# Last scatters waited for on SyncE, one weight subtraction on VectorE, half of the expert bias loaded in the expert stage, and the end of the second attention in another order

## The reference

```python
x = x + _L0_xattn_ref(_layernorm(x), ctx_4096, ctx_4096, ...)   # 8 heads over 64 rows of a batch
x = x + _L0_ffn_ref(_layernorm(x), L0_ffn_W_gate, L0_ffn_b_gate, L0_ffn_W_e, L0_ffn_b_e)
x = x + _L1_xattn_ref(_layernorm(x), ctx_4096, ctx_4096, ...)   # 32 heads, 8 key heads
x = x + _L1_ffn_ref(_layernorm(x), ...)                         # gated, 1376 hidden
```

```python
logits = x @ W_gate + b_gate
_, top_idx = jax.lax.top_k(logits, TOP_K)          # TOP_K = 2
y_all = relu(einsum('bsd,edh->bseh', x, W_e) + b_e)
y = take_along_axis(y_all, top_idx[..., None], axis=2).mean(axis=2)
```

## Time and profile before

| what | value |
|---|---|
| median of 3 runs | 890.0 us (886.49 to 892.05) |
| the profiled execution | 889.12 us |
| its span in the trace | 887.4 us |
| mean granted clock | 0.985 of full speed |
| busy share of PE, DVE, ACT, POOL | 95%, 49%, 39%, 32% |
| PE's share of the chain that ended last | 73% |

### The profile page before, as it was taken

One profiled execution on the slowest core, in us unless ns is written; L12 is line 12 of the kernel. 1 busy time (PEld: TensorE's weight loads), 2 busy tenths in 40 slices (PEclk: granted clock), 3 DMA queues, 4 the chain that ended last, 5 costly groups with the idle time before them and its releaser, 6 DMA issues.

```text
span 887.4 us, 19751 instructions
## 1 busy us (share of the span) xinstructions
...
## 2 busy tenths in 40 slices
...
GB/s 284 131 252 254 229 251 288 171 322 199 166 164 113 197 122 135 170 143 144 118 50 58 137 119 38 45 33 1 18 114 12 1 13 107 0 49 47 1 0 48
DMA packets 55388, 105.28 MB, mean 119 GB/s; under 512 B 8226, under 2 KB 12322, under 8 KB 55042
## 3 DMA queue, kind: packets, MB, share of 16 engines
...
## 4 chain that ended last, share of the span: by engine, by line
PE 73%; POOL 3%; issue 2%; DMA 2%; ACT 1%; DVE 1%; SPq 0%; DVEq 0%; ACTq 0%; POOLq 0%
PE c_ps L1273 9%; PE c_ps L1275 9%; PE c_ps L1274 9%; PE c_bank L1797 4%; PE c_bank L1311 3%; PE c_bank L1312 3%; PE c_bank L1317 3%; PE c_bank L1798 3%; PE c_bank L1803 3%; PE c_bank L1861 3%; PE c_bank L1010 2%; PE c_bank L1011 2%; PE c_bank L1016 2%; PE c_ps L1836 2%; PE c_po L1011 2%
## 5 line engine op out<-in xcount | busy, mean ns | idle before, releaser
L1350 DVE SCALAR_TENSOR_TENSOR d_hid<-c_ps,d_b_up,d_silu 128x512 f32<-128x512 f32 (+1 forms) x44 | 33.0, 751 | 227.9 <-PE c_ps L1275 227.9
L1273 PE MATMUL c_ps<-d_nT_hi,gate_up_hi 128*128 128x512 f32 (+1 forms) x352 | 139.9, 398 | 0.0
L1275 PE MATMUL c_ps<-d_nT_hi,gate_up_lo 128*128 128x512 f32 (+1 forms) x352 | 138.6, 394 | 0.0
L1274 PE MATMUL c_ps<-d_nT_lo,gate_up_hi 128*128 128x512 f32 (+1 forms) x352 | 138.3, 393 | 0.0
L1229 ACT ACTIVATE d_silu<-c_ps,d_b_gate 128x512 f32<-128x512 f32 (+1 forms) x44 | 30.3, 689 | 141.6 <-PE c_ps L1275 141.6
L1189 POOL TENSOR_TENSOR late_x<-late_x,d_b_down 128x512 f32<-128x512 f32 x16 | 20.9, 1340 | 188.8 <-DMA late_x<-x_after_attention 188.8
L1275 PEld LDWEIGHTS c_ps<-d_nT_hi,gate_up_lo 128*128 128x128 f32 (+1 forms) x352 | 65.2, 185 | 16.6
L1274 PEld LDWEIGHTS c_ps<-d_nT_lo,gate_up_hi 128*128 128x128 f32 (+1 forms) x352 | 65.4, 186 | 15.9
L1273 PEld LDWEIGHTS c_ps<-d_nT_hi,gate_up_hi 128*128 128x128 f32 (+1 forms) x352 | 65.3, 185 | 15.4
L1236 ACT ACTIVATE d_hid_hi<-d_hid 128x512 fp32r<-128x512 f32 (+1 forms) x44 | 27.8, 632 | 125.4 <-DVE d_hid L1350 125.4
L1040 ACT ACTIVATE b_rowsT_hi<-c_bank 128x512 fp32r<-128x512 f32 x39 | 23.4, 599 | 77.8 <-PE c_bank L999 77.8
...
## 6 DMA issues: line engine op xcount, KB each, us to landing
...
```

Source lines behind the costliest of these rows:

```text
L1273: pe.matmul(bank[0:w, :], gu_hi[:, cols], nT_hi[:, g % 2, k, :], start=k == 0, stop=False)
L1274: pe.matmul(bank[0:w, :], gu_hi[:, cols], nT_lo[:, g % 2, k, :], start=False, stop=False)
L1275: mm = pe.matmul(bank[0:w, :], gu_lo[:, cols], nT_hi[:, g % 2, k, :], start=False, stop=k == KD - 1)
```

## The change

- At the start SP issues the six loads of the output projection's constants (`load_o_consts`, L288 to L291) before, no longer after, the loads of ctx(1) and x(2).
- bias(0) is no longer loaded in the first block. SP issues it in the expert stage between the loads of the rows of blocks 1 and 2. bias(1) stays where it is.
- The wait for the last scatters moves from the end of POOL's part of the first block to the end of SP's.
- The low part of the last piece of expert weights is made by DVE (`last_low_part`), at step m == TILES between the marks of tile 13 and the residual of tile 15.
- POOL scatters tile 12 after the scaling of tile 15's norm and the marks of tile 13; before it did so ahead of both.
- At the end of the second attention PE does the low product of tile 13 after attend of tile 14's second half. DVE adds tile 13's projection one step later, and divides tile 14's first half before it takes maxima of tile 15.
- DVE does `low_weights(3)` one step later.

```diff
--- before.py
+++ after.py
@@ -318,9 +318,9 @@
             load_ctx(0)
             load_x(1)
             load_v_consts()
+            load_o_consts()
             load_ctx(1)
             load_x(2)
-            load_o_consts()
             load_weights(0)
             load_ctx(2)
             load_gate_consts()
@@ -335,16 +335,12 @@
                 want(sp, kv_made, i - 2)
                 sp.dma_start(ctx_in[(i + 1) % 3], late["ctxT"][KV_EARLY + i, :, :]).then_inc(ctxT_loaded[i % 3], 16)
 
-            def load_bias(half):
+            def load_bias():
                 sp.wait_ge(o_made, TILES)
-                if half:
-                    sp.wait_ge(w_lo, TILES)
-                else:
-                    sp.wait_ge(y_made, TILES)
-                    sp.wait_ge(l_made, TILES)
-                cols = slice(half * EXPERTS * DIM // 2, (half + 1) * EXPERTS * DIM // 2)
+                sp.wait_ge(w_lo, TILES)
+                cols = slice(EXPERTS * DIM // 2, EXPERTS * DIM)
                 rows = shared["b_e"].rearrange("e h -> (e h)")[cols].partition_broadcast(P)
-                sp.dma_start(shared["bias"][:, cols], rows).then_inc(shared["bias_loaded"][half], 16)
+                sp.dma_start(shared["bias"][:, cols], rows).then_inc(shared["bias_loaded"][1], 16)
 
             def store_kv(i):
                 sp.wait_ge(kv_kept, i + 1)
@@ -376,14 +372,13 @@
                 if i + 3 < KV_LATE:
                     load_ctxT(i + 3)
                 if i == 2:
-                    load_bias(1)
-                if i == 5:
-                    load_bias(0)
+                    load_bias()
                 store_kv(i)
             sp.wait_ge(ctxT_loaded[(KV_LATE - 1) % 3], 16 * ((KV_LATE - 1) // 3 + 1))
             sp.wait_ge(front_zeroed, 16)
             for i in range(2):
                 sp.wait_ge(x1_stored[i], 8 * TILES)
+                sp.wait_ge(scattered[i], 16 * TILES)
 
         @block.gpsimd
         def _(pool):
@@ -444,20 +439,18 @@
                                             in_=xn2[:, t % KEPT, :], in_offset=None).then_inc(scattered[t % 2], 16)
 
             for m in range(-2, TILES + 4):
-                if m >= TILES and tile(m - 4):
+                if m > TILES and tile(m - 4):
                     scatter(m - 4)
                 if tile(m + 2) or tile(m - 1):
                     scale_rows(m)
-                if tile(m - 1):
+                if tile(m - 1) and m < TILES:
                     if tile(m - 3):
                         pool.wait_ge(both_ready, m - 2)
                     low_part(m - 1)
                 if 0 <= m - 3 < TILES - SEEN_LATE:
                     add_seen(pool, m - 3)
-                if m < TILES and tile(m - 4):
+                if m <= TILES and tile(m - 4):
                     scatter(m - 4)
-            for i in range(2):
-                pool.wait_ge(scattered[i], 16 * TILES)
 
         @block.scalar
         def _(act):
@@ -779,6 +772,12 @@
                 dve.wait_ge(xn_ready, t + 1)
                 dve.scalar_tensor_tensor(x[t % RING], pvy[:, :], bo[:, 0:1], x[t % RING], ALU.add, ALU.add).then_inc(x1_ready, 1)
 
+            def last_low_part():
+                dve.wait_ge(w_hi, TILES)
+                dve.wait_ge(w_lo, TILES - 1)
+                high, low = expert_weights(TILES - 1)
+                dve.tensor_tensor(low, wstage[:, (TILES - 1) % 2, :], high.bitcast(F32), ALU.subtract).then_inc(w_lo, 1)
+
             def sum_x1(t):
                 dve.wait_ge(x1_ready, t + 1)
                 dve.bn_stats(stats2[:, t % 2, :], x[t % RING]).then_inc(norm2_step, 1)
@@ -851,6 +850,8 @@
                 if tile(m - 3):
                     mark_experts(m - 3)
                     add_marks(m - 3)
+                if m == TILES:
+                    last_low_part()
                 if tile(m - 1):
                     add_residual(m - 1)
                 if tile(m + 1):
@@ -977,6 +978,9 @@
         for b in range(BLOCKS + 6):
             if b < BLOCKS:
                 load(b)
+            if b == 1:
+                cols = slice(0, EXPERTS * DIM // 2)
+                sp.dma_start(bias[:, cols], b_e.rearrange("e h -> (e h)")[cols].partition_broadcast(P)).then_inc(shared["bias_loaded"][0], 16)
             if b == 3:
                 sp.wait_ge(kv_kept, 1)
                 sp.dma_start(shared["kv"][last, :, :], kv_stage[:, 0:KV_COLS]).then_inc(last_stored, 16)
@@ -1910,6 +1914,8 @@
                 if 0 <= m - 1 < TILES:
                     attend(m - 1, 1, 0)
                     attend(m - 1, 1, 1)
+                if m == TILES - 1:
+                    project_low(m - 2)
                 if m + 1 < TILES:
                     make_q(m + 1)
                 if m in (0, TILES - 1):
@@ -1933,7 +1939,7 @@
                     scores(m + 1, 0)
                     transpose_probs(m, 1, 0)
                     transpose_probs(m, 1, 1)
-                if 0 <= m - 1 < TILES:
+                if 0 <= m - 1 < TILES and m != TILES - 2:
                     project_low(m - 1)
                 if m == TILES - 1:
                     pe.wait_ge(s_shifted, 2 * TILES)
@@ -2050,7 +2056,7 @@
             keep_values(7)
             keep_low_x(1)
             for m in range(TILES + 2):
-                if 0 <= m - 2 < TILES:
+                if 0 <= m - 2 < TILES and m != TILES - 1:
                     add_attn(m - 2)
                 if m < TILES - 1:
                     max_scores(m, 0)
@@ -2060,6 +2066,8 @@
                 if 0 <= m - 1 < TILES:
                     invert_sums(m - 1, 1)
                     keep_attn(m - 1, 1)
+                if m == TILES - 1:
+                    add_attn(m - 2)
                 if m == 1:
                     sum_x2(3)
                     average_x2(3)
@@ -2067,6 +2075,8 @@
                     sum_x3(m - 2)
                 if 0 <= m - 1 < TILES:
                     turn_attn(m - 1, 1)
+                if m == 1:
+                    low_weights(3)
                 if 0 <= m - 2 < TILES and m != TILES - 1:
                     average_x3(m - 2)
                 if m < TILES:
@@ -2080,20 +2090,18 @@
                 if m == TILES - 1:
                     sum_x3(m - 2)
                     average_x3(m - 2)
+                if m < TILES:
+                    invert_sums(m, 0)
+                    keep_attn(m, 0)
                 if m == TILES - 2:
                     max_scores(m + 1, 0)
                     shift_scores(m + 1, 0)
-                if m < TILES:
-                    invert_sums(m, 0)
-                    keep_attn(m, 0)
                 if m and m + 3 < TILES:
                     sum_x2(m + 3)
                 if m < TILES:
                     turn_attn(m, 0)
                 if m and m + 3 < TILES:
                     average_x2(m + 3)
-                if m == 0:
-                    low_weights(3)
                 if m == TILES - 1:
                     for n in range(TG):
                         ffn.keep_first_low(dve, n)
```

## The result

The changed kernel takes 884.78 us (median of 18 runs, 882.66 to 889.08), the kernel before 890.24 (18 runs). The ratio is 0.9943, with a 95% interval of 0.9924 to 0.9961, which is 5 us. The profiled execution took 884.15 us, with a span of 882.4 and a granted clock of 0.989. The forecast was 887.0 in a range of 881.5 to 891.5. The time lies in the range, but the terms of the sum did not come out, and that their total did is luck: the start cost nothing, the boundary gave 4.1 of the 5.0 us forecast and lost most of them again, and the end of the second attention gave about three quarters of the whole (0.7 us forecast, about 4 measured).

What follows compares the result with a forecast made beforehand. It took PE, full from 24 to 120 us, as the bound. +1.7 - 2.6 - 2.4 + 1.0 - 0.7 = -3.0 on the profiled 889.1 gave 886.1, and 0.9 for the median 887.0 us, range 881.5 to 891.5.

Steps and rivals of the forecast that it cites:

- the boundary: End of the first block: POOL's DRAIN starting sooner, 2.6 us, and the last scatters ending sooner, 2.4 us, both gains.
- Start: Start of the kernel: x(2) lands 4.1 us later, 2.1 of it hidden; cost 1.7 us, between 0 and 3.7.
- the slack behind x(3): At the start, tile 0's sums wait for x(3) until 19.7, 2.1 us after attend(0), hiding that much delay.
- Behind it PE is full, so it stays: After the start: PE has no idle time to absorb the 1.7 us loss, so it reaches the end in full.
- DRAIN: End of the first block: with the wait on SP, POOL drains while scatters fly; gain 2.6 us, between 0 and 2.68.
- the DRAIN waits for POOL's DMAs: Rival at the end of the first block: wherever the DRAIN stands; sum -0.4, 889.6 us, chance 0.07.
- the later block: Evidence on the DRAIN: one there ended 2.69 us behind POOL's last work, with no DMA of POOL's in sight.
- Scatters sooner: End of the first block: last issue 0.6 us sooner and flight 4.8 instead of 6.6; gain 2.4 us, between 0 and 5.
- bias(0) in the expert stage: Expert stage: its 1 MB lies ahead of block 2's rows and delays them; cost 1.0 us, between 0 and 2.5.
- Second attention: End of the second attention: PE's 1.37 us wait before attend(14)'s second half goes; gain 0.7 us, between 0 and 2.
- DVE decides: End of the second attention: DVE is full from 487.75 to 492.94, and shedding two operations there sets the gain, 0.7 us.

Runs made afterwards that it cites:

- pool_low: The changed kernel with the last weight subtraction on POOL and tile 12's scatters ahead of the scaling of tile 15's norm, both as before; 884.32 us, ratio 0.9946.
- bias_later: The changed kernel with bias(0) issued behind the rows of block 2 instead of ahead of them; 882.03 us, ratio 0.9908.
- wait_pool: The changed kernel with the wait for the last scatters at POOL's end again instead of SP's; 884.76 us, ratio 0.9936.

## Why the prediction held, and where it did not

- **Start, +1.7; measured 0.** That x(2) would go out at 12.1 was right (12.07), and so was the slack behind x(3). The mis-sized step is its flight: I took 4.5 us, and it was read 3.0 us after its issue, at 15.08 and not 16.6. With 3.0 my own working gives attend(0) at 20.15, where it ended, and a cost of 0.4; the sums of tile 0 were inverted 0.35 later. "Behind it PE is full, so it stays" failed too. I counted time at the full clock only, though the row of K at half the clock (1.92 us at 22.09) stood in the same view.
- **DRAIN, -2.6; measured -1.6.** The rival "the DRAIN waits for POOL's DMAs" had half of it: it can't end ahead of them, but it ends 1.35 behind their landing and not 2.9. I read the later block rightly, but it has no DMA of POOL's, so it could not tell a fixed price from a wait for them.
- **Scatters sooner, -2.4; measured -2.5** (155.45 to 152.22 in landing, less the 0.7 of the start in that profile), by bias(0); the order of POOL's work and the subtraction had no part in it that shows (pool_low). The nearness is luck: with bias(0) there, two other profiles have the landing at 158.39 and 159.49. With the DRAIN's 1.6 that makes 4.1, and the first product came 4.1 sooner, for 5.0 forecast.
- **bias(0) in the expert stage, +1.0; measured 1.2 of wait, but at another place:** PE's wait of 1.16 is for the rows of block 1, with whose transfer the bias shares the DMA engines, not for block 2's. With bias_later 0.8 of it goes.
- **Missing from the sum: the clock behind the barrier.** The work behind it starts 4.8 us sooner, and its first products now fall into the low clock. Of 4.1 us gained between 28 and 155 us (4.8 less the start's 0.7), 1.0 is left at block 1. How much of it a run keeps depends on when the clock falls and how long it stays low: in the fourteen profiles 3.4 to 13.7 us around the barrier, from code that hardly differs there. That this is what levels the times of wait_pool and the changed kernel is read from one profile of each; more of them would be needed to call it shown.
- **Second attention, -0.7; measured -4.1 in the profile** (-3.8 from the scores to the end). The failed step is "DVE decides". The 0.7 was the right size for what it priced: PE starts attend(15) 0.74 us sooner. Left out were the 2.11 us stop in attend(15) and the half clock behind it, 496.0 to 499.4, which are 3.3 us. I took them as given because the profile names no releaser. In the changed kernel PE came to attend(14)'s second half ahead of SP's burst, its load of instructions was not held up, and both went.

The total held because the errors had both signs, which is luck. In the trace's own terms the start came out 2.4 us better than forecast (0.7 gained for 1.7 lost), the boundary with bias(0) 3.0 worse (1.0 gained up to block 1 for 4.0), the stretch from there to 487 us 0.5 worse, the end of the second attention 3.4 better (4.1 for 0.7), and what follows 0.2 worse.
